# A second layer on sorted (token, expert) pairs, 44 steps of 128 rows, in place of all eight experts for every token

## What is computed

```
x = x + layer1(layernorm(x))   # 4 experts, one for each token, by its token id;
                               # one 512 x 512 matrix C[e] serves as gate, up and down:
                               # y = (silu(h C^T) * (h C^T)) C^T
x = x + layer2(layernorm(x))   # 8 experts of hidden size 64, each with a LoRA pair of rank 16:
scores = softmax(h @ G)        # 512 x 8
value, indices = top_k(scores, 2)          # two experts for each token
gate = silu(h @ gate_w[e].T); up = h @ up_w[e].T
out = sum over the two: value * ((gate * up) @ down_w[e].T + (h @ lora_A[e].T) @ lora_B[e].T)
```

## Time and profile before

| | |
|---|---|
| Profiled execution: time, and its span | 331.94 us, 330.1 us |
| TensorE busy (x instructions) | 304.6 us, 92% (x1636) |
| VectorE busy | 212.8 us, 64% (x603) |
| ScalarE busy | 82.9 us, 25% (x158) |
| GpSimd busy | 108.7 us, 33% (x118) |
| DMA moved | 26.37 MB, mean 80 GB/s |
| Granted TensorE clock, mean | 0.986 |

### The profile page before, as it was taken

The page is one execution under the profiler, slowest core; times in us unless marked ns, Lnnn a source line. Parts: engine busy times, 40 slices in busy tenths (PEclk is TensorE's granted clock), DMA queues, the critical chain, the costliest instruction groups (busy, mean ns, idle before and its releaser), DMA issues.

```text
span 330.1 us, 5390 instructions
## 1 busy us (share of the span) xinstructions
PE 304.6 (92%) x1636; PEld 269.1 (82%) x1637; DVE 212.8 (64%) x603; ACT 82.9 (25%) x158; POOL 108.7 (33%) x118
## 2 busy tenths in 40 slices
PE   1649997999999999999999999999999999999990
PEld 1636885888888888889999999999999999999970
DVE  7879865674666576467865686658756776557520
ACT  3523213232332323231212211221212121212110
POOL 1779834566566445431120111101110111011111
PEclk9979999999999999999999999999999999999996
DMA  7462685122212323222210122011110000000000
GB/s 252 164 213 73 165 318 213 70 95 71 90 64 95 95 64 115 75 64 65 66 64 0 64 64 64 14 50 64 64 38 26 32 32 32 0 32 34 32 28 37
DMA packets 8074, 26.37 MB, mean 80 GB/s; under 512 B 1408, under 2 KB 1408, under 8 KB 7424
## 3 DMA queue, kind: packets, MB, share of 16 engines
q0 software_dynamic: 4320, 14.16, 12.5%
q1 hardware_dynamic: 3744, 12.08, 11.3%
HBM read 17.06 MB, written 9.18 MB: 79 GB/s over the span
## 4 chain that ended last, share of the span: by engine, by line
PE 81%; POOL 6%; DMA 6%; issue 2%; DVE 2%; ACT 0%; DVEq 0%; ACTq 0%; POOLq 0%
PE p_y L681 10%; PE p_y L686 10%; PE p_y L682 10%; PE p_h L681 7%; PE p_h L686 7%; PE p_h L682 7%; PE p_aT L676 5%; PE p_xT L670 4%; PE p_a L682 3%; PE p_a L681 3%; PE p_a L686 3%; PE p_b L682 3%; PE p_b L686 3%; PE p_b L681 3%; DMA xin<-x,gather_row 3%
## 5 line engine op out<-in xcount | busy, mean ns | idle before, releaser
L492 DVE TENSOR_TENSOR aT_lo<-p_aT,aT_hi 128x512 fp32r<-128x512 f32 (+1 forms) x35 | 26.3, 752 | 85.8 <-ACT aT_hi L320 83.1
L253 POOL DMA_INDIRECT out<-xout,out_row x16 | 16.6, 1035 | 134.8 <-DVE xout L500 133.1
L320 ACT ACTIVATE aT_hi<-p_aT 128x512 fp32r<-128x512 f32 (+1 forms) x35 | 22.7, 648 | 106.2 <-PE p_aT L676 100.1
L253 POOL DMA_INDIRECT x_rows<-xout,x_row x19 | 19.7, 1038 | 55.0 <-DVE xout L500 54.7
L681 PE MATMUL p_y<-ctx_hi,aT_hi 128*128 x76 | 31.4, 414 | 2.5 <-DVE xout L500 2.4
L681 PE MATMUL p_y<-w_hi,aT_hi 128*128 128x512 f32 x75 | 30.7, 410 | 0.0
L682 PE MATMUL p_y<-ctx_lo,aT_hi 128*128 x76 | 29.8, 392 | 0.0
L681 PE MATMUL p_h<-ctx_hi,xT_hi 128*128 x72 | 29.8, 413 | 0.0
L682 PE MATMUL p_y<-w_lo,aT_hi 128*128 128x512 f32 x75 | 29.4, 393 | 0.0
L682 PE MATMUL p_h<-ctx_lo,xT_hi 128*128 x72 | 28.3, 392 | 0.0
L247 POOL TENSOR_TENSOR rstd<-var_eps,neg_half 128x1 f32<-128x1 f32 x35 | 23.1, 659 | 13.0 <-DVE var_eps L475 12.9
(11 more groups left out here) (145 smaller groups left out, 663.5 us busy)
## 6 DMA issues: line engine op xcount, KB each, us to landing
whole<-ctx_t SPq DMA_DIRECT2D x4, 1024.0 KB, 6.5
xin<-x_rows SPq DMA_DIRECT2D x16, 256.0 KB, 2.6
whole<-w_up SPq DMA_DIRECT2D x4, 580.0 KB, 5.1
whole<-w_down SPq DMA_DIRECT2D x1, 1280.0 KB, 8.0
xin<-x,gather_row POOLq DMA_INDIRECT x19, 3.4
x_rows<-xout,x_row POOLq DMA_INDIRECT x19, 3.1
out<-xout,out_row POOLq DMA_INDIRECT x16, 2.9
ids<-token_ids SPq DMA_DIRECT2D x1, 8.0 KB, 1.6
```

The lines of the kernel that those rows point to most:

```text
L253: nc.gpsimd.indirect_dma_start(out=to, out_offset=bass.IndirectOffsetOnAxis(ap=rows, axis=0), in_=xout[:, r % 2, :], in_offset=None).then_ ...
L320: nc.scalar.activation(aT_hi[:, 0:cols], p_aT[:, 0:cols], ACT.Copy).then_inc(ahi_ready, 1)
L492: nc.vector.tensor_tensor(aT_lo[:, 0:cols], p_aT[:, 0:cols], aT_hi[:, 0:cols].bitcast(F32), ALU.subtract).then_inc(alo_ready, 1)
```

## The change

Layer 2 no longer computes all experts. Each token yields two pairs, (token, lower expert) in phase A and (token, higher expert) in phase B. During layer 1 each finished tile t goes to a record buffer `rec` (a ring of eight). It is centred, transposed, and multiplied in fp32 with the router matrix (`turn_x2`, `route`); DVE picks the two experts (`choose`), and for batches of four tiles computes one-hots and gate weights (`owners`, `places`) and, with f16 matmuls (`rank`, `total`), the row of each pair in a region for its expert. POOL scatters each record twice (`scatter`), into the DRAM tensors `rows_a` and `rows_b`, with reciprocal deviation, mean, weight and target row beside its 512 features. When the first 16 tiles are ranked, `early_list` names the first 7 pair steps of phase A (full tiles only), and after the last batch `whole_lists` names the rest; `fill_region` writes 128 empty rows behind each region. Each phase then has 22 steps of 128 rows of one expert. A pair step loads its rows (SP, `load_pair`, a ring of six buffers), transposes, multiplies by that expert's 288 columns (gate, up, LoRA A, each in two parts), gates, transposes 80 columns, and multiplies three times 80x512. Phase A scatters x + weight x result into `sums_b` at the pair's row of phase B, and phase B adds to it and scatters to `out`. The ring `xin` has six buffers instead of eight; the sort of layer 1 no longer makes a second, compact order. The `Fori` loops are unrolled.

```diff
+NB = E2 - 1; CAP = TOKENS + P; META = 4; EARLY = 7
+PHASE = TILES + NB - 1; PAIRS = 2 * PHASE
+XRING, RRING = 6, 8
+ARING, YRING, ORING = 6, 4, 4
+BATCHES = [(0, 4), (4, 8), (8, 12), (12, 16), (16, 19)]
...
 # SP
+            def load_pair(s):
+                if s >= ARING:
+                    sp.wait_ge(stored[(s - ARING) % ORING], 16 * ((s - ARING) // ORING + 1))
+                row = sp.value_load(pair_row[0:1, s:s + 1], min_val=0, max_val=DUMMY)
+                rows = rows_a if s < PHASE else rows_b
+                sp.dma_start(pair_x[:, s % ARING, :], rows[bass.ds(row, P), :]).then_inc(pair_landed[s % ARING], 16)
...
+            for s in range(ARING):
+                load_pair(s)
+            sp.wait_ge(lists_ready, 2)
+            for e in range(NB):
+                fill_region(0, e)
+            for s in range(ARING, EARLY):
+                load_pair(s)
+            ...
+            for s in range(EARLY, PAIRS + 3):
+                ...
+                if s < PAIRS:
+                    load_pair(s)
+                if s - 3 == PHASE:
+                    ... # waits for every store of phase A
+                if s - 3 >= PHASE:
+                    load_sum(s - 3)
+                if EARLY + 2 <= s < EARLY + 2 + NB:
+                    fill_region(1, s - EARLY - 2)
...
 # POOL, step k of layer 1
+                if k + 3 < STEPS: inverse_deviation(k + 3)
+                if 0 <= k - 2 < STEPS and k + 4 < STEPS: gather(k + 4)
+                if k >= 2: inverse_deviation2(k - 2)
+                if PIECE0 <= k < PIECE0 + PIECES: split_lo(k - PIECE0)
+                ... # scatter of four records in k = 7 + 4b and 8 + 4b, phases 0 and 1
...
 # ACT, step k
+                hi_act(k - 1); centre(k - 2); l1_silu(k); hi_x(k + 1); copy_x2T(k - 2)
+            def centre(t):
+                sc.wait_ge(stats2_ready, t + 1)
+                nc.scalar.activation(record(t), record(t), ACT.Identity, bias=neg_mean2[:, t:t + 1]).then_inc(xc_ready, 1)
...
 # DVE, step k
+                lo_act(k - 1); residual(k - 2)          # residual now ends with bn_stats of the record
+                statistics(k + 3, between=k + 2)
+                statistics2(k - 2)                      # bn_aggr, -mean, variance + eps -> stats2_ready
+                choose(k - 3)
+                if (k - 3) % 4 == 3: owners((k - 3) // 4)
+                l1_gate(k); lo_x(k + 1)
+                if (k - 3) % 4 == 3: places((k - 3) // 4)   # after the fourth batch also early_list()
...
 # PE, step k
+                turn_act(k - 1)
+                l1_first(k)
+                turn_x(k + 1)
+                turn_x2(k - 2)                          # waits for xc_ready
+                if k >= 6 and (k - 6) % 4 == 0: rank((k - 6) // 4)
+                l1_second(k - 1)
+                route(k - 2)
...
 # one iteration i of the pair steps, on each engine
+  PE:   up(i); ta(i - 1); down(i - 2); tx(i + 2)
+  ACT:  copy_b(i); ah2(i - 1); gate_silu(i); hi2(i + 2); mean_back(i)   # mean_back in phase A alone
+  DVE:  combine(i); al2(i - 1); gate_up(i); pair_finish(i - 2); lo2(i + 2)
+  POOL: store(s) for each s, waits for pair_done
+            def up(s):
+                e = pair_matrices(s)                    # value_load of pair_expert
+                ...
+                for i in range(KB):                     # 288 columns: w_hi and w_lo side by side
+                    nc.tensor.matmul(to[:, 0:2 * UP], xT_hi[:, s % 2, blk(i)], up_w[:, bass.ds(e + i * E2, 1), :, :]...)
+                pe.wait_ge(lo2_ready, s + 1)
+                for i in range(KB):                     # 144 columns
+                    last = nc.tensor.matmul(to[:, 0:UP], xT_lo[:, s % 2, blk(i)], up_w[:, bass.ds(e + i * E2, 1), 0, :]...)
+            def pair_finish(s):
+                if s >= ORING:
+                    dve.wait_ge(stored[s % ORING], 16 * (s // ORING))
+                dve.wait_ge(o_ready, s + 1)
+                ... # other: x1_pair in phase A, pair_sum in phase B
+                nc.vector.scalar_tensor_tensor(pair_out[:, s % ORING, :], p_o[s % 2][:], pair_meta(s, GATE), other,
+                                               ALU.mult, ALU.add).then_inc(pair_done, 1)
...
 # DVE, between the layers
+            lo_act(STEPS - 1); residual(STEPS - 2); statistics2(STEPS - 2); choose(STEPS - 3)
+            lo2(0); lo2(1); residual(STEPS - 1); choose(STEPS - 2); statistics2(STEPS - 1)
+            pair_iteration(0); choose(STEPS - 1); owners(4)
+            pair_iteration(1); places(4)
+            pair_iteration(2); whole_lists()
```

More of the change, by code:

```diff
@@ L96, in build @@
[L96 to L100, removed]
+        xT_hi, xT_lo = (sb(n, [P, 2, D], F32R) for n in ("xT_hi", "xT_lo"))
+        x2T = sb("x2T", [P, D])
+        act = sb("act", [P, D])
+        aT_hi, aT_lo = (sb(n, [P, D], F32R) for n in ("aT_hi", "aT_lo"))
@@ new lines, in pair_iteration @@
+            def pair_iteration(i):
+                if i < PAIRS:
+                    combine(i)
+                if 0 <= i - 1 < PAIRS:
+                    al2(i - 1)
+                if i < PAIRS:
+                    gate_up(i)
+                if 0 <= i - 2 < PAIRS:
+                    pair_finish(i - 2)
+                if i + 2 < PAIRS:
+                    lo2(i + 2)
+            split_ctx(0, 0)
+            split_ctx(1, 0)
+            statistics(0)
+            statistics(1, between=0)
@@ new lines, in _ @@
+            lo_act(STEPS - 1)
+            residual(STEPS - 2)
+            statistics2(STEPS - 2)
+            choose(STEPS - 3)
+            lo2(0)
+            lo2(1)
+            residual(STEPS - 1)
+            choose(STEPS - 2)
+            statistics2(STEPS - 1)
+            pair_iteration(0)
+            choose(STEPS - 1)
+            owners(len(BATCHES) - 1)
+            pair_iteration(1)
+            places(len(BATCHES) - 1)
+            pair_iteration(2)
+            whole_lists()
+            for i in range(3, PAIRS + 2):
+                pair_iteration(i)
@@ new lines, in route @@
+            def route(t):
+                c = t % 2 * E2
+                pe.wait_ge(x2T_out, t + 1)
+                if t == 0:
+                    pe.wait_ge(route_landed, 16)
+                    pe.wait_ge(rows_ready, 3)
+                if t >= 1:
+                    pe.wait_ge(logits_out, t)
+                for i in range(KB):
+                    last = nc.tensor.matmul(p_rt[:, c:c + E2], x2T[:, blk(i)], route_w[:, i * E2:(i + 1) * E2],
+                                            start=(i == 0), stop=(i == KB - 1))
+                last.then_inc(logits_ready, 1)
@@ L773, in _ @@
[L773 to L784 removed]
+                turn_x(1)
@@ new lines, in _ @@
+            turn_act(STEPS - 1)
+            turn_x2(STEPS - 2)
+            l1_second(STEPS - 1)
+            route(STEPS - 2)
+            tx(0)
+            tx(1)
+            turn_x2(STEPS - 1)
+            pe.wait_ge(w2_lo_ready, PIECES)
+            pair_iteration(0)
+            route(STEPS - 1)
+            pair_iteration(1)
+            total(len(BATCHES) - 1)
+            rank(len(BATCHES) - 1)
+            pair_iteration(2)
+            for i in range(3, PAIRS + 2):
+                pair_iteration(i)
```

1209 lines of the change are left out of this document (721 added, 488 removed).

## The result

The changed kernel takes **472.6 us** (median of 4 runs, 468.6 to 477.0) against 332.1 us (4 runs, 330.9 to 333.4): 1.419 times as long, 95% interval [1.406, 1.432]. The ratio is that of the three fast runs, 468.6 to 473.8 us, without the fourth, the profiled one, which took 476.99 us for a span of 475.2 and lies 1.8% above the fastest. Forecast were 415 us in a range of 352 to 447. The sign was right, the size was not: 57.6 us are missing.

A forecast was written before the change was run, and what follows sets the result against it. TensorE's matmuls were taken to bound the kernel before. Forecast: 202 us to step 18, 67 for the change of phase, 132 for pair steps, 4.5 between phases, 7.8 at the end, 1.8 around: 415 us, range 352 to 447.

The forecast's parts named there:

- part 1: Steps of layer 1: PE waits for ACT's centring, a step goes from 6.41 to 10.4 us, step 18 starts at 202.
- part 2: Change of phase: lists, fills and loads without cover, `pair_finish(3)` ends 67 us after the start of step 18.
- part 3: Pair steps: the six-buffer ring's chain of 9.95 us over three steps gives 3.3 us each, 132 us for 40.
- the end: From the last DVE result to the end of span: stays 7.8 us.
- (d): Rival: TensorE's clock at the half level, a pair step's PE work 4.1 us, 447 us in all; chance 0.05.
- the change from `rows_a` to `rows_b`: Between the pair phases: `load_sum(22)` waits for the store of pair 21, adding 4.5 us.
- (a): Rival: layer 1 does not stall, PE's 8.0 us of work bound its step, 374 us in all; chance 0.12.
- (b): Rival: the ring of six buffers doesn't bind pair steps, DVE sets 2.4 us each, 376 us in all; chance 0.11.
- (c): Rival: software pipelines hide every latency, each stretch goes by its busiest engine, 300 us in all; chance 0.12.

The follow-up runs named there:

- e4: Changed kernel, with 28 discarded matmuls on PE before the wait for the centred tile in layer-1 steps: 456.2 us, 1.372 of the kernel before.
- e2: Changed kernel with eight pair buffers instead of six: 415.7 us, 1.250 of the kernel before.
- e1: Changed kernel, with PE doing `turn_x2` after `l1_second` and `route` one step later in layer 1: 430.3 us, 1.294 of the kernel before.
- e9: Changed kernel with seven pair buffers instead of six: 431.9 us, 1.301 of the kernel before.
- e6: Changed kernel with `turn_x2` later, eight pair buffers, lists before the first pairs, SP's value load before its store wait: 362.6 us, 1.090 of the kernel before.
- e3: Changed kernel, with 16 discarded matmuls on PE before the wait for each pair's rows, from pair 6 on: 470.6 us, 1.415 of the kernel before.
- e5: Changed kernel, with DVE finishing step 18 and the lists before the first pairs, ACT and PE following: two runs, 450.9 and 463.3 us.
- e11: Kernel before, with `bounds_check` and `oob_is_err=False` added to its stores: 333.6 us, 1.000 of the kernel before.

## Why the prediction was wrong

By its own sum, 202 + 67 + 132 + 4.5 + 7.8 + 1.8. The profiled run is 61.9 us over it, 9.4 in part 1, 9.4 in part 2, 39.2 in part 3 and 3.9 at the end:

**Part 1, right in mechanism and in size.** The stall is where it was put, 2.07 us for 2.5, the step 10.49 for 10.4; `route` takes 0.81 us until the next `turn_act` for 0.9; the centring takes 0.72 for 0.6 and loads no table. Step 18 starts at 211.5 and not at 202. The 9.4 us are the clock: e4 gives them back. That the rest meets the forecast to 0.3 us is in part luck: step 2 started at 33.7 as before and not at 32, and steps 16 and 17 were 1 us short of the rest. The prediction argued that a gap of 2.5 us leaves the clock alone, from a single gap near 50 us, after a stretch in which PE was full. In plain steps it often did (1.00 between 90 and 122 us), but not in the batch steps and not in every plain step, and the price was in no term: (d) counted the half level in the pair steps alone.
The Trainium skill, "TensorE: Matmul & The Clock Gate", section "A second HAM failure mode: psum-queue depth-cycling", says that short idles between groups of matmuls make the clock go back and forth. This trace agrees in that the clock goes back and forth where PE stands still for short times: 0.93 over 60 to 200, 0.72 over 290 to 400. It also has 32 us with a wait of 2.07 us in each step at 1.00. The prediction gave (d) 0.05.

**Part 2, right in order, 9 us short.** 76.4 us for 67. The first `up` came at 35.7 for 32, the lists at 54.4 for 52, the load of pair 6 at 68.2 where some 60 was forecast. The seven fills took 13.2 us to issue and not 7.7. Five of them went at the forecast 1.1 us or little more; between 266.8 and 273.3 SP's sequencer needed some 0.7 us for each of its small steps that otherwise take 0.02 to 0.33. The lines of the fills, and the first of them in e2 (duration in ns: min, median, max):

```profile
L275 SPq FUSED_REGOPS  x14: 3/152/727, 266.4 to 321.8; - x14
L275 SPq SEQ_ASSERT  x14: 18/18/706, 266.6 to 322.0; - x14
...
L281 SPq FUSED_REGOPS  x14: 152/152/159, 261.7 to 299.0; - x14
```

What holds SP there no run shows, and it is found in this run alone: in e1 to e9 no register operation, move or issue of the fills takes longer than 0.36 us, and the seven fills took 9.0 us in e6 and 9.6 in e2. Without it some 72 us would stand for the 67, as in e2 and e3. e5 shows that 11 to 15 of the 76 us were order alone, which the prediction saw (`lo2(0)` ahead of `residual(18)`) and took as given.

**Part 3 is the step that failed**, "Sum 9.95, **3.3 us per step**": the chain is the right one, as the table of ring sizes shows, but three steps of it take 13.1 us (phase A) and not 9.95, a pair step 4.35 and not 3.3. With the change from `rows_a` to `rows_b`, 175.7 us came for 132 + 4.5. That is 39 of the 61.9 us. Against the turn shown above: store landing 2.7 for 2.9, SP 0.73 for 0.65, load 2.67 for 2.6 and finish 0.8 for 0.75 were right. Wrong were POOL's part, 0.79 for 0.3, since the row it was taken from had no bounds check (e11); the transposes, 1.15 for 0.65, at the half level; and the stretch from the transposes to the finish, 3.33 for 2.1. There the prediction followed DVE's order (`hi2`, `lo2`, `combine`, `gate_silu`), while the chain goes through PE's, which has first to do `up`, `ta` and `down` of the pairs before; part of the 3.33 is the half level, since the turn of e3 at the full one needs 2.81 there, with waits in it. The landings get longer in other turns: on the chain from 290 to 440 us a store takes 3.5 us on average and a load 3.0, together 1.1 more than in the turn shown, which makes 13.1 out of 12.2. The upper bound of 3.8 per step took in long landings and none of the rest. For the change from `rows_a` to `rows_b` 4.5 us were forecast; the turn with it, `pair_finish(21)` to `(24)`, takes 16.3 us, 3.4 more than three other steps.

**The end**, 11.7 us for 7.8: POOL's closing drain is 8.3 us long where it was 4.5.

**Rivals.** (a) and (b) are refuted by the two stalls, (c), 300 us, by the time; and even e6, without the stall and with the longer ring, is 30 us slower than the kernel before. (d) was half right: the half level is there, and costs 4.6 to 9.7 us in layer 1 and 0 to 18 in the pair steps. The range failed because it took in one shortfall at a time, where clock, check, PE's order, landings and drain all went the same way. They weren't independent: the longer the waits on the ring, the lower the clock (the table), and the slower the matmuls in the next turn.

## What to carry to other kernels

Where a ring of buffers closes over a DMA round trip, price a turn by what the engine in the middle does in its program order, not by what the data needs, and try the number of buffers first: two more took the pair step from 4.39 to 3.04 us here, 54 us in all. A stall that comes back in every step is also a question to the clock, so price the work around it at both of its levels. When work moves behind lists that the kernel computes itself, put the lists ahead of everything that doesn't need waiting for: here their first operation had its input at about 233.6 and started at 243.0, behind a load that it never read.

## What had not been expected of the hardware

- A scatter with a bounds check starts 0.79 us after DVE's result, without one 0.28 us after it (e11); off the path it costs nothing (1.000 [0.995, 1.005]).
- POOL's drain at the end takes 4.475 us after the 54 indirect DMAs of the kernel before and 8.313 us after the 101 of the changed one, 0.082 to 0.083 us for each; e6 has 101 as well, and 8.313 us. Two counts are all that these runs have.
- With nothing but the number of buffers changed, the granted clock of the pair steps went from 0.60 to 0.72, 0.85 and 0.97. Shorter waits on the ring gave the clock back; the clock alone, raised by dropped matmuls, brought next to nothing (e3).
- A register load on SP takes 0.27 us at the median. The Trainium skill, "DMA: Bandwidth & Descriptors", section "Latency and other measured facts", gives a floor of about 600 ns for a `tensor_load`, which is what the trace calls this instruction; the 44 of `load_pair` in this trace go from 262 to 718 ns with a median of 268, below that floor.
